# Second layer's attention: query and value as three-term products of parts from the fourth batch on; first layer's attention: the gate's product ahead of the transposes

## The reference, cut to what matters

```
q, k, v = silu(h @ Wq), silu(h @ Wk), silu(h @ Wv)      # 16 heads of 16
o       = decayed causal linear attention of q, k, v
gate    = (h @ Wg1) @ Wg2                               # rank 16
og      = o * sigmoid(gate), then a norm per head       # rsqrt of the mean square
y       = (og * norm_w) @ Wo
```

```
q, k = h @ Wq, h @ Wk          # 32 heads of 8
v    = h @ Wv                  # 16 heads of 16
aw   = softmax(causal(q @ k.T * scale)); aw = aw[even heads] - lam * aw[odd heads]
attn = rmsnorm(aw @ v) * (1 - lambda_init)
y    = attn @ Wo
```

## Time and profile before

| what | value |
|---|---|
| median of 3 runs | 1938.45 us (1938.06 to 1944.51) |
| the profiled execution's own time | 1938.25 us |
| its span, first to last instruction | 1936.1 us |
| PE busy | 1699.5 us, 88% of the span |
| DVE, POOL, ACT busy | 1379.9, 922.0, 763.3 us |
| mean granted clock of TensorE | 0.948 of full |
| first layer's attention | about 30 to 356 us of the span |
| second layer's attention | about 586 to 1131 us of the span |

### The profile page before, as it was taken

One profiled execution on the slowest core, in us unless ns is written; L12 is line 12 of the kernel. 1 busy time (PEld: TensorE's weight loads), 2 busy tenths in 40 slices (PEclk: granted clock), 3 DMA queues, 4 the chain that ended last, 5 costly groups with the idle time before them and its releaser, 6 DMA issues.

```text
span 1936.1 us, 41184 instructions
## 1 busy us (share of the span) xinstructions
PE 1699.5 (88%) x14072; PEld 1215.0 (63%) x14072; DVE 1379.9 (71%) x3608; ACT 763.3 (39%) x1538; POOL 922.0 (48%) x968
## 2 busy tenths in 40 slices
PE   6999999699996999999999978889966788999886
PEld 3666665599993555555555546667655666888443
DVE  5888888476654675766666668888845776888686
ACT  5555554122232556565655541111122212444442
POOL 2576766565552446454645353332234222666343
PEclk8999998799997999999999999999999888999997
DMA  7000000100016554646455300000011000000011
GB/s 263 12 18 11 17 17 7 34 13 10 9 22 125 137 112 90 114 82 117 90 106 102 73 7 15 9 10 8 9 33 46 15 14 22 9 17 14 31 49 52
DMA packets 70580, 93.84 MB, mean 48 GB/s; under 512 B 10424, under 2 KB 64808, under 8 KB 67240
## 3 DMA queue, kind: packets, MB, share of 16 engines
q1 hardware_dynamic: 70456, 92.15, 20.7%
HBM read 61.84 MB, written 29.49 MB: 47 GB/s over the span
## 4 chain that ended last, share of the span: by engine, by line
PE 55%; DVE 23%; issue 9%; POOL 6%; ACT 4%; DMA 1%; DVEq 1%; SPq 1%; ACTq 0%; POOLq 0%
PE PS L1137 17%; PE PS L2151 4%; PE PS L2241 3%; DVE negmax L2479 3%; PE PS L2115 3%; PE PS L1326 3%; POOL l_ms L1099 3%; DVE rt_eq L1516 2%; ACT pw L2394 2%; DVE xn L527 2%; PE PS L537 2%; PE PS L2176 2%; DVE st L506 2%; PE PS L2135 2%; PE PS L2254 1%
## 5 line engine op out<-in xcount | busy, mean ns | idle before, releaser
L2479 DVE TENSOR_REDUCE negmax<-PS 128x2 f32<-128x512 f32 (+1 forms) x384 | 247.1, 685 | 173.1 <-PE PS L2151 167.4
L568 POOL TENSOR_TENSOR X<-X,y_sb 128x512 f32 (+1 forms) x128 | 164.5, 1285 | 120.5 <-DVE y_sb L563 115.4
L547 ACT ACTIVATE hT<-PS,modT 128x256 f32<-128x256 f32 x256 | 130.2, 560 | 128.5 <-PE PS L537 126.7
L1137 PE MATMUL PS<-we_hi,h_parts 128*128 128x512 f32 x512 | 177.4, 406 | 1.7 <-POOL h_parts L1608 1.6
L2394 ACT ACTIVATE pw<-PS 128x512 f32<-128x512 f32 x256 | 139.2, 601 | 74.1 <-PE PS L2151 74.1
L563 DVE TENSOR_TENSOR y_sb<-PS,ga_sb 128x512 f32<-128x512 f32 x96 | 66.2, 689 | 134.1 <-PE PS L2688 43.5
L527 DVE TENSOR_SCALAR xn<-X,mv,rs 128x256 f32 (+1 forms) x256 | 139.7, 587 | 6.1 <-POOL rs L520 4.7
L1137 PE MATMUL PS<-l_h_parts,lut_hi 128*128 128x256 f32 (+1 forms) x704 | 132.9, 290 | 7.4 <-POOL l_h_parts L1291 7.4
L518 POOL TENSOR_TENSOR rs<-mv,eps 128x2 f32<-128x2 f32 x128 | 26.7, 209 | 203.3 <-DVE mv L511 203.1
L1702 DVE SCALAR_TENSOR_TENSOR l_acc<-PS,rt_g,l_acc 128x256 f32<-128x256 f32 x256 | 105.8, 475 | 20.9 <-PE PS L1137 20.7
L1137 PEld LDWEIGHTS PS<-l_h_parts,lut_hi 128*128 128x128 f32 (+1 forms) x704 | 109.7, 190 | 10.2 <-issue 5.4
(11 more groups left out here) (300 smaller groups left out, 4346.2 us busy)
## 6 DMA issues: line engine op xcount, KB each, us to landing
ga_sb<-ga_dram SPq DMA_DIRECT2D x128, 128.0 KB, 2.9
qk_dram<-qk_parts SPq DMA_DIRECT2D x64, 192.0 KB, 2.8
KS<-qk_dram SPq DMA_DIRECT2D x32, 384.0 KB, 5.8
QS<-qk_dram SPq DMA_DIRECT2D x32, 384.0 KB, 8.8
qk_dram<-qk_parts SPq DMA_DIRECT2D x64, 128.0 KB, 2.8
wmod<-in_wmod SPq DMA_DIRECT2D x4, 1536.0 KB, 12.9
qk_dram<-qk_parts SPq DMA_DIRECT2D x64, 64.0 KB, 2.5
y_out<-X SPq DMA_DIRECT2D x16, 256.0 KB, 2.2
```

Of the source, the lines that this page charges most:

```text
L547: last_ = act.activation(hT[b.par][:, kh, :], PS[:, 0, kh * T:(kh + 1) * T], ACT.Identity, bias=modT[:, sub, 0, kh, bass.ds(b.n, 1)], scal ...
L568: pool.tensor_tensor(xb(b), xb(b), y_sb[b.par][:, :, :], ALU.add).then_inc(s.x.sem, 1)
L1137: last_ = pe.matmul(out, x.bitcast(F32R), y.bitcast(F32R), start=start and n == 0, stop=stop and n == 2)
L2479: dve.tensor_reduce(to, src, AX.X, ALU.max, negate=True).then_inc(s.max.sem, 1)
```

## The change

Two edits.

First attention: on TensorE `project_gate(i)` moves ahead of `normed_T(d)`; on ACT the tanh of the gate moves ahead of the copy `ogT`.

Second attention: for batches 3 to 15 the query and value products are made by `matmul3` from float32r parts, twelve matmuls in the place of eight records; the key product stays as it is. For it, ACT writes the high part of h for every batch from 1 on (`h_hi`, a copy of 128x512), POOL the low part (`h_lo`, a subtraction of 128x512) as the first long step of its slot, and DVE forms the parts of the two weights once, at the end of slot 1 (two copies and two subtractions of 128x512). `project_q` waits for `h_lo` and the weights' parts. New buffers: `l1_w_hi`, `l1_w_lo`, `l1_h_parts` (one buffer, so `h_hi(b)` waits until `project_v(b-1)` has read it).

```
                 ahead(ln_transpose, pe, pl, i, 1)
+                if i.ok:
+                    project_gate(i)
                 if d.ok:
                     normed_T(d, i)
-                if i.ok:
-                    project_gate(i)
                 if c.ok:
                     values(c, 1)
...
                     act.activation(l0a_h_parts[(i + 1).par][:, 0].bitcast(F32R), hT[(i + 1).par][:, :, :], ACT.Copy).then_inc(s.h_hi.sem, 1)
+                if i.ok:
+                    act.wait_ge(*s.gate_ps(i))
+                    if d.ok:
+                        act.wait_ge(*s.u(d))
+                    act.activation(gate[i.par][:, :, :].rearrange("p t d -> p (t d)"), bank(1), ACT.Tanh, scale=0.5)\
+                       .then_inc(s.gate.sem, 1)
                 if d.ok:
                     act.wait_ge(*s.ogT_ps(d))
...
-                if i.ok:
-                    act.wait_ge(*s.gate_ps(i))
...
+            def in_parts(b):
+                return b.off >= 3
+
             def project_q(b):
                 pe.wait_ge(*s.k(b))
-                project_T(b, "q", s.q_ps)
+                if not in_parts(b):
+                    project_T(b, "q", s.q_ps)
+                    return
+                pe.wait_ge(*s.h_lo(b))
+                pe.wait_ge(setup["w_lo"], 5)
+                for m in range(KH):
+                    for kh in range(KH):
+                        last_ = matmul3(pe, bank(0)[:, m * T:(m + 1) * T],
+                                        [w["q"][:, kh, m * P:(m + 1) * P] for w in (l1_w_hi, l1_w_lo)],
+                                        [l1_h_parts[:, part, kh, :] for part in range(2)], kh == 0, kh == 1)
+                last_.then_inc(s.q_ps.sem, 1)
...
+                        if in_parts(b):
+                            last_ = matmul3(pe, bank(0)[:, t * D:(t + 1) * D],
+                                            [l1_h_parts[:, part, kh, t * P:(t + 1) * P] for part in range(2)],
+                                            [w["v"][:, kh, :] for w in (l1_w_hi, l1_w_lo)], kh == 0, kh == 1)
+                        else:
+                            last_ = pe.matmul(bank(0)[:, t * D:(t + 1) * D], hT[b.par][:, kh, t * P:(t + 1) * P],
+                                              l1_w["v"][:, kh, :], start=kh == 0, stop=kh == 1)
...
+            def h_hi(b):
+                first_ = b.reg is None and b.off == 1
+                act.wait_ge(*s.h(b))
+                if first_:
+                    if pl:
+                        act.wait_ge(*sigs[pl - 1].y(Idx(None, B - 1)))
+                else:
+                    act.wait_ge(*s.hfree(b - 1))
+                act.activation(l1_h_parts[:, 0].bitcast(F32R), hT[b.par][:, :, :], ACT.Copy).then_inc(s.h_hi.sem, 2 if first_ else 1)
...
                 if d.ok:
                     exps(d, 1, 2)
+                if c.ok and i.ok:
+                    h_hi(c)
                 if c.ok and not first_done(c):
                     evict_qk(c, 1, s.k_ps, s.k, 1.0)
...
+            def weight_parts():
+                for n in "qv":
+                    split_hi(dve, l1_w_hi[n][:, :, :], l1_w[n][:, :, :]).then_inc(setup["w_hi"], 1)
+                for k, n in enumerate("qv"):
+                    dve.wait_ge(setup["w_hi"], 4 + k)
+                    dve.tensor_tensor(l1_w_lo[n][:, :, :].bitcast(F32R), l1_w[n][:, :, :], l1_w_hi[n][:, :, :], ALU.subtract)\
+                       .then_inc(setup["w_lo"], 1)
...
                 if d.ok:
                     mean_square(d)
+                if i.reg is None and i.off == 1:
+                    weight_parts()
...
+            def h_lo(b):
+                pool.wait_ge(*s.h_hi(b))
+                pool.tensor_tensor(l1_h_parts[:, 1].bitcast(F32R), hT[b.par][:, :, :], l1_h_parts[:, 0], ALU.subtract)\
+                    .then_inc(s.h_lo.sem, 2 if b.reg is None and b.off == 1 else 1)
...
+                if (i + 1).ok and i.ok:
+                    h_lo(i + 1)
                 if (i + 1).ok and not (pl and i.reg is None and i.off == -1):
                     l1a_split(pool, s, i + 1, 1, 0)
                     l1a_split(pool, s, i + 1, 0, 2)
```

More of the change, by code:

```diff
@@ L249, in build @@
                         "msplit": 6, "mparts": 2, "mT_ps": 2, "mT": 2, "score": 24, "prob": 24, "pv": 4, "oT": 4,
-                        "otok_ps": 4, "rl": 4, "u": 4, "att": 1, "sq": 1, "ms": 1, "rn_raw": 1, "rn": 1, "og": 1,
+                        "h_hi": 1, "h_lo": 1, "otok_ps": 4, "rl": 4, "u": 4, "att": 1, "sq": 1, "ms": 1, "rn_raw": 1, "rn": 1, "og": 1,
                         "ogT_ps": 1, "ogT": 1, "y_ps": 1},
@@ L444, in build @@
         l1_og, l1_ogT = sb("l1_og", [P, TT, D], F32, work), sb("l1_ogT", [P, KH, T], F32, work)
+        l1_w_hi, l1_w_lo = ({n: sb(f"l1_w{n}_{part}", [P, KH, D], F32, work) for n in "qv"} for part in ("hi", "lo"))
+        l1_h_parts = sb("l1_h_parts", [P, 2, KH, T], F32, work)
         work.close()
@@ L953, in slot @@
                     act.activation(l0a_h_parts[(i + 1).par][:, 0].bitcast(F32R), hT[(i + 1).par][:, :, :], ACT.Copy).then_inc(s.h_hi.sem, 1)
[L954 to L958, removed]
                 if i.ok:
@@ L964, in slot @@
                        .then_inc(s.gate.sem, 1)
+                if d.ok:
+                    act.wait_ge(*s.ogT_ps(d))
+                    if (d - 1).ok:
+                        act.wait_ge(*s.y_ps(d - 1))
+                    act.activation(ogT_sb[:, :, :].rearrange("p k t -> p (k t)"), bank(2), ACT.Copy).then_inc(s.ogT.sem, 1)
                 if c.ok:
@@ L2134, in project_v @@
                     for kh in range(KH):
-                        last_ = pe.matmul(bank(0)[:, t * D:(t + 1) * D], hT[b.par][:, kh, t * P:(t + 1) * P],
-                                          l1_w["v"][:, kh, :], start=kh == 0, stop=kh == 1)
+                        if in_parts(b):
[5 more added lines that the diff above has]
+                                              l1_w["v"][:, kh, :], start=kh == 0, stop=kh == 1)
                 last_.then_inc(s.hfree.sem, 1)
```

## The result

The changed kernel takes 1917.61 us in the median of four executions (1914.06 to 1918.67), beside 1940.20 for the kernel before (four, 1938.06 to 1944.51): ratio 0.9878, 95% interval 0.9854 to 0.9901. In a later comparison it took 1915.42 beside 1940.85 (0.9869, 0.9846 to 0.9891). The prediction was 1918, with a range from 1911 to 1927. The execution shown here took 1914.06 us with a span of 1912.3, 23.8 less than the span of 1936.1 before. In the changed kernel's text all lines of the first attention stand two further down (L846 is L848 now, and so on).

A forecast was written before the change was run, and what follows sets the result against it. First attention was taken as bound by a chain of waits mostly through POOL, with DVE's work close behind; second attention by PE. Gains 13.9 + 6.9 - 0.5 = 20.3 us off 1938.25 gave 1918, range 1911 to 1927.

The forecast's parts named there:

- Gate product first: First attention: gate product fills PE's 0.90 us idle, `out` comes earlier, most clock falls go; 13.9 us over twelve intervals.
- the new interval: First attention: y_sb to y_sb, bounded by 17.40 and 17.95 us, taken as 17.6 instead of 18.76 in the mean.
- The clock: First attention: PE's falls to 1.2 GHz in every other slot, 1.62 us each, expected mostly to go with the idle wait.
- most falls go: First attention: most clock falls disappear once PE's idle wait is filled; counted within the 13.9 us.
- the idle wait: First attention: PE's 0.90 us wait for POOL ahead of `normed_T`, taken as part of what precedes each clock fall.
- rival 1: First attention: the clock falls stay, gain there only 7.5 us, time 1924.4; chance 0.18.
- Query and value products: Second attention: float32r parts save 0.31 us on q and 0.8 x 0.28 on v per slot; 6.9 us over 13.
- What hides the new work: Second attention: `h_hi` fits ACT's idle time, `h_lo` on POOL ends 1.5 us before `project_q`, stack has room; cost nothing.
- Weights' parts: End of slot 1: four DVE instructions, 2.8 us in all, where DVE idles 3.49; cost 0.5 us, at most 1.9.
- Total: Whole kernel: 13.9 + 6.9 - 0.5 = 20.3 us gained, from 1938.25 to 1918.

The follow-up runs named there:

- e5: Kernel before, with eight full-height float32r products filling TensorE's idle time ahead of the normed output's transposes, gate order unchanged; 1930.81 us beside 1940.29.
- e3: Kernel before, with the gate's product issued once more in TensorE's idle time ahead of `normed_T`, real product left in place; 1940.61 us beside 1938.87.
- e6: Changed kernel, with the gate's product issued twice in a row ahead of the normed output's transposes; 1930.46 us beside 1940.29 for the kernel before.
- e4: Kernel before plus the second attention's edit, but query and value products stay float32: parts formed and waited for, not used; 1938.36 us beside 1938.87.
- e2: Kernel before plus the second attention's edit alone, first attention unchanged; 1933.15 us beside 1938.87.
- e7: Changed kernel, with DVE issuing the first attention's y_sb behind the first of four bit extractions, not all four; 1930.16 us beside 1940.29 for the kernel before.
- e8: Changed kernel, with second attention's key products in parts too and both input parts formed on DVE; 1912.45 us beside 1940.85 for the kernel before.
- e1: Kernel before plus the first attention's edit alone, on TensorE and ACT; 1920.97 us beside 1938.87.
- e10: Kernel before plus the first attention's edit on TensorE only, ACT's order unchanged; 1921.87 us beside 1940.85.

## Why the prediction was right, point by point

- *Gate product first*: forecast 13.9 us, measured 225.12 - 208.05 = 17.1 in the changed kernel (16.6 when it was run again). Sign, place and order of size were right. The term that was mis-sized is the new interval, put at 17.6: it is 17.34, below the 17.40 that I had named as its end. The reason given for 17.6 (y_sb is held by DVE's own queue) is right: no y_sb has a wait ahead of it any more. But DVE too gained: in the same 208 us its idle time fell from 28.9 to 16.3. That the scores that come earlier are the reason is likely and was not tested.
- *The clock*: "most falls go" came true, all six went, and 1.62 us a fall was nearly right (9.5 / 6 = 1.58 by e5). The cause that I gave, the idle wait, is refuted by e3: with the idle time filled by a product of a 16-row operand the falls stay, and by e5 they go when it is filled by full-height float32r products. That the falls went was luck as far as my reason goes: the move of the gate's product also shortens the stretch from 3.2 us to 2.2. In e6, with the new order but the stretch at 3.1 us, five falls are there: the case of rival 1, but for the doubled product.
- *Query and value products*: forecast 6.9, measured 13 x 0.60 = 7.8. q's 0.31 came as 0.30. For v I let only 0.8 of 0.28 arrive, by the waits of the last slot; v saved 0.30 and all of it arrived. The waits for the maxima stayed at 15.0 and 2.6 us: TensorE's whole stream moves up, DVE's with it.
- *What hides the new work*: right, by e4. `project_q` doesn't wait for `h_lo`, and no TensorE wait for the stack appears.
- *Weights' parts*: forecast 0.5 with 1.9 as its end, measured nothing: the slot takes 35.31 to 35.40 us in the kernels that form them and have the same 6.83 us at half clock in it (e2, e4, e6, e7, e8, and the changed kernel run again), and 35.21 to 35.39 in those that don't form them (before, e1, e5, e10). The two DVE copies took 0.42 and 0.46 us, not the 1.63 of the earlier trace rows. The case that I priced, the copies beside the power of 5.44 us, did not occur: they ended at 641.73, and the power began at 642.57. The rule of the Trainium skill, SBUF — State Buffer, section "SBUF: two separate sides", is that DVE (in a two-port mode, or with two inputs in SBUF) and GpSimd hold a shared pair of ports as an exclusive lock: whichever starts first keeps it for its whole instruction, and the other waits. The trace agrees with it in both directions: the first copy ended at 641.36, 0.29 us behind the end of the POOL step begun at 640.83 (641.07), and POOL's addition, begun at 641.80, took 0.69 us in the place of 0.25 and ended 0.11 behind DVE's subtraction (642.38). The power, begun beside the second subtraction, took 5.77 in the place of 5.44.
- *Total*: 17.1 + 7.8 = 24.9; the profiled spans differ by 23.8, the medians by 22.6 and 25.4. By the two traces the changed kernel is ahead by 16.7 us at the last y_sb of the first attention, by 14.2 at the block of k behind the slot with the weights' parts (which holds the additional 3.41 us at half clock), by 21.4 at the last block of k, by 21.2 at the last y_sb of that stage and by 23.8 at the end. The last 2.6 us come in stages that the change doesn't touch, where the clock's falls lie elsewhere. The prediction had no term for them, and they set how finely changes of this kernel can be told apart.

## What to carry to other kernels

Where TensorE's granted clock drops at a regular place, look at the kind of work there, not at its idle time alone: a row of transposes and products of a 16-row operand was as costly here as the same row with a gap in it, and breaking it with full-height float32r work brought back 9.5 us. When an engine is busy for 92% of a stage, an operation moved up in its queue pushes all that it passes, so list who waits for each of these before moving it, and look at what it lets another engine start: e7's y_sb released a POOL step that then held DVE for 1.10 us. The savings on TensorE in the second attention arrived whole, 0.60 of 0.60 us and 0.17 of 0.18, and its waits there are nearly all for DVE's maxima, which TensorE itself feeds.

## What the runs showed of the hardware that was not expected

- TensorE's clock fell to 1.2 GHz right behind 3.41 us in which the engine was busy throughout (e3), and stayed at 2.4 GHz with the same order and eight float32r products of 128x128 by 128x256 in the gap (e5).
- A float32r product in a block of twelve costs 1.53 / 12 to 1.75 / 12 = 0.13 to 0.15 us, a float32 one of the same shape 1.83 / 4 = 0.46. So three parts are cheaper than one float32 product only by 0.18 to 0.30 us in a block of 1.9, and the same block cost 1.53 us for v, 1.63 for q and 1.75 for k, by what stands around it.
- DVE's extraction of 128x268 int32 takes 0.29 us, but 0.85 or 1.39 when a POOL instruction has got in ahead of it: it then ends 0.16 us behind POOL's, in the changed kernel and in e7 alike. The other way round, POOL's step on 128x268 took 1.17 us instead of 0.75 at 148.76 us in the changed kernel, where no extraction was held. No run was made with POOL's step moved away.
